# Joined column halves, a halved last tile and new order tables in a three-stage transformer block on one core

## The reference

```python
x = L0_attn_a_x                                   # (4, 512, 512) float32
# 1: sparse layer
attn = einsum('ds,td->st', w1, w2) * sparse_mask
x = x + gelu(einsum('bds,st->bdt', layernorm(x), attn) + b2)
# 2: clustered layer
n = layernorm(x)
dots = softmax(n @ centroids.T / 0.1);  hits = dots > 0.01
query_sel = any(hits, axis=1);  row_sel = any(hits, axis=0)[assignments]
x = x + where(query_sel[:, None] & row_sel[None, :], n @ weight.T + bias, 0)
# 3: attention with one head of 128
q, k, v = split(layernorm(x) @ Wqkv + bqkv)
x = x + softmax(q @ k.T / sqrt(128)) @ v @ Wo + bo
# 4: the clustered layer again, with the same weights
```

## Time and profile before

| | us |
|---|---|
| median of 3 runs | 284.21 |
| lowest, highest | 283.50, 284.87 |
| the profiled execution's own time | 283.48 |
| its span in the profile | 281.7 |
| TensorE busy | 271.4 (96%) |
| VectorE busy | 229.5 (81%) |
| ScalarE busy | 150.8 (54%) |
| GpSimd busy | 147.4 (52%) |

### The profile page before, as it was taken

One profiled execution on the slowest core, in us unless ns is written; L12 is line 12 of the kernel. 1 busy time (PEld: TensorE's weight loads), 2 busy tenths in 40 slices (PEclk: granted clock), 3 DMA queues, 4 the chain that ended last, 5 costly groups with the idle time before them and its releaser, 6 DMA issues.

```text
span 281.7 us, 4762 instructions
## 1 busy us (share of the span) xinstructions
PE 271.4 (96%) x1596; PEld 235.6 (84%) x1596; DVE 229.5 (81%) x458; ACT 150.8 (54%) x274; POOL 147.4 (52%) x186
## 2 busy tenths in 40 slices
PE   6999999999999999999799999999999999999893
PEld 5878888888888898789789999999889988898672
DVE  2889798968977958678799888889658796896996
ACT  5476747434757474264686665871653555356300
POOL 2233770485952554579999998671073005305820
PEclk9999999999999999999999999999999999999999
DMA  6985939000000000000000000000000000000087
GB/s 223 376 332 181 357 122 349 23 0 3 0 0 3 0 0 2 0 0 3 0 1 2 0 2 0 0 3 0 2 1 0 2 0 2 1 0 5 0 300 296
DMA packets 9976, 18.26 MB, mean 65 GB/s; under 512 B 1056, under 2 KB 1568, under 8 KB 9952
## 3 DMA queue, kind: packets, MB, share of 16 engines
q1 hardware_dynamic: 9952, 17.96, 18.0%
HBM read 13.76 MB, written 4.19 MB: 64 GB/s over the span
## 4 chain that ended last, share of the span: by engine, by line
PE 79%; POOL 8%; DVE 6%; issue 4%; ACT 1%; DVEq 1%; POOLq 0%; ACTq 0%
PE m_bank L864 60%; PE t_bank L955 11%; PE m_bank L1025 5%; POOL y_tok L480 3%; DVE x_tok L848 3%; POOL y_tok L493 2%; POOL rstd L431 1%; PE m_bank L856 1%; PE m_bank L915 1%; PE t_bank L961 1%; POOL ve L430 1%; DVE y_tok L841 1%; DVE odd_lo L707 1%; DVE st L700 1%; POOL nbias L434 1%
## 5 line engine op out<-in xcount | busy, mean ns | idle before, releaser
L700 DVE BATCH_NORM_STATS2 st<-x_tok 128x6 f32<-128x512 f32 x64 | 43.6, 681 | 0.5 <-DMA x_tok<-in_L_attn_a_x 0.4
L493 POOL TENSOR_TENSOR y_tok<-y_tok,x_tok 128x512 f32<-128x512 f32 x16 | 20.9, 1329 | 38.3 <-ACT y_tok L649 38.3
L864 PE MATMUL m_bank<-ffn_hi,even_hi 128*128 128x512 f32 x96 | 39.2, 408 | 0.0
L864 PE MATMUL m_bank<-ffn_lo,even_hi 128*128 128x512 f32 x96 | 37.6, 391 | 0.0
L864 PE MATMUL m_bank<-ffn_hi,even_lo 128*128 128x512 f32 x96 | 37.5, 391 | 0.0
L430 POOL TENSOR_SCALAR ve<-mv 128x1 f32<-128x1 f32 (+1 forms) x31 | 9.2, 297 | 39.3 <-DVE mv L701 37.7
L473 POOL TENSOR_TENSOR y_tok<-y_tok,bias_f 128x512 f32<-128x512 f32 x16 | 20.6, 1300 | 16.6 <-ACT y_tok L594 16.6
L864 PE MATMUL m_bank<-odd_hi,wqkv_hi 128*128 128x256 f32 x96 | 27.8, 290 | 1.1 <-ACT y_tok L594 1.1
L864 PE MATMUL m_bank<-odd_lo,wqkv_hi 128*128 128x256 f32 x96 | 27.1, 283 | 0.0
L864 PE MATMUL m_bank<-odd_hi,wqkv_lo 128*128 128x256 f32 x96 | 27.1, 282 | 0.0
L431 POOL TENSOR_TENSOR rstd<-ve,half 128x1 f32<-128x1 f32 (+1 forms) x31 | 23.6, 762 | 2.6
(11 more groups left out here) (163 smaller groups left out, 791.6 us busy)
## 6 DMA issues: line engine op xcount, KB each, us to landing
out<-x_tok SPq DMA_DIRECT2D x16, 256.0 KB, 2.3
x_tok<-in_L_attn_a_x SPq DMA_DIRECT2D x3, 1024.0 KB, 11.3
xn_odd<-in_L_attn_a_xt SPq DMA_DIRECT2D x2, 1024.0 KB, 6.1
w_raw<-in_L_attn_a_w SPq DMA_DIRECT2D x4, 256.0 KB, 4.2
y_tok<-in_L_attn_a_w SPq DMA_DIRECT2D x4, 256.0 KB, 4.4
x_tok<-in_L_attn_a_x SPq DMA_DIRECT2D x2, 512.0 KB, 6.6
y_tok<-in_L_attn_a_sparse_mask SPq DMA_DIRECT2D x1, 1024.0 KB, 9.2
xt_other<-in_L_ffn_weight SPq DMA_DIRECT2D x1, 1024.0 KB, 11.3
```

The source lines that it names most:

```text
L493: pool.tensor_tensor(y_tok[:, n, :], y_tok[:, n, :], x_tok[:, n, :], ALU.add).then_inc(done[kind], 1)
L700: link(dve.bn_stats(st[:, at % 2, :], x_tok[:, n, :]))
L864: ins = pe.matmul(bank, a, w, start=(first and n == 0), stop=(last and n == count - 1))
```

## The change

It does six things.

- For q, k and v of batches 1 to 3, pv of all batches, and the cluster products of batches 0 to 2 in both clustered stages, the two halves become one step `h01`: 12 (cluster: 8) products of 512 columns for 24 (16) of 256, waiting for all four tiles.
- The last dense tile, batch 3 tile 3 of stage 4, becomes two steps `dn4h` of 256 output columns, each with its own bank, `blend4h`, `outh` and store.
- All tables of TensorE, ScalarE, VectorE and GpSimd are new. SyncE's differs only in the last store.
- `WARM` is 4.
- `logit` waits for the count of `prob` that its own batch has in the table, since the two orders may differ.
- `rq` gets a leading dimension of 2, of which the second half is used; the `mT` names stand for no step.

```diff
-WARM = 6
+WARM = 4
...
 PE_ORDER = """
-T.v.0.0 k.1.h0 q.1.h0 q.1.h1 T.p.0.0 T.p.0.1 T.p.0.3 T.p.0.2 k.1.h1 v.1.h1 v.1.h0 sc.1.3 pv.0.h1 sc.1.1 T.x3.2.2
...
+k.1.h01 q.1.h01 T.p.0.3 T.p.0.1 T.p.0.2 v.1.h01 T.x3.2.0 T.x3.2.1 sc.1.0 sc.1.2 sc.1.1 T.x3.2.2 sc.1.3 T.x3.2.3
...
-store.2.2 store.2.3 store.3.0 store.3.1 store.3.2 store.3.3
+store.2.2 store.2.3 store.3.0 store.3.1 store.3.2 storeh.3.3.0 storeh.3.3.1
...
@@ -149,12 +149,12 @@
 PARTS = {"y1": KC, "dn2": KC, "dn4": KC, "cl2": 2, "cl4": 2, "q": 2, "k": 2, "v": 2, "pv": 2, "colmean": KC}
 T_KINDS = ("T", "tc", "bestT", "colmean")
-M_KINDS = ("last", "y1", "dn2", "dn4", "cl2", "cl4", "q", "k", "v", "sc", "pv", "wo", "mask")
+M_KINDS = ("last", "y1", "dn2", "dn4", "dn4h", "cl2", "cl4", "q", "k", "v", "sc", "pv", "wo", "mask")
 def tile_of(kind, key):
-    return () if kind == "colmean" else key[:-1] if kind in PARTS else key
+    return () if kind in ("colmean", "mT") else key[:-1] if kind in PARTS else key
 def products_order():
@@ -169,7 +169,7 @@
             first.add(at)
             rotating = [t for t in bank if (t[0] in T_KINDS) == (kind in T_KINDS)]
             bank[tile] = len(rotating)
-        taken[tile] += 1 if kind not in PARTS or kind == "colmean" else len(str(key[-1])) - 1
+        taken[tile] += 1 if kind not in PARTS or kind in ("colmean", "mT") else len(str(key[-1])) - 1
         if taken[tile] == PARTS.get(kind, 1):
             last.add(at)
     return first, last, bank
@@ -281,7 +281,7 @@
         csum = sb("csum", [P, TPB])
         crec = sb("crec", [P, TPB])
         qsel = sb("qsel", [P, 2, NT])
-        rq = sb("rq", [P, NT])
+        rq = sb("rq", [P, 2, NT])
         t_bank = [ctx.enter_context(nc.psum_tensor(f"t_bank{i}", [P, 512], F32)) for i in range(T_BANKS)]
         m_bank = [ctx.enter_context(nc.psum_tensor(f"m_bank{i}", [P, 512], F32)) for i in range(M_BANKS)]
@@ -354,6 +354,12 @@
                     b, t = key
                     sp.wait_ge(*done_at("out", (b, t)))
                     sp.dma_start(out_d[b, t * P:(t + 1) * P, :], x_tok[:, b * TPB + t, :]).then_inc(stored, 16)
+                    continue
+                if kind == "storeh":
+                    b, t, h = key
+                    cols = slice(h * D // 2, (h + 1) * D // 2)
+                    sp.wait_ge(*done_at("outh", key))
+                    sp.dma_start(out_d[b, t * P:(t + 1) * P, cols], x_tok[:, b * TPB + t, cols]).then_inc(stored, 16)
                     continue
                 what = key[0]
                 if what in ("w2", "w1"):
@@ -395,7 +401,7 @@
                     sp.wait_ge(*done_at("alo"))
                     sp.dma_start(wqkv_raw, rows_of(wqkv_d)).then_inc(ld[key], 16)
                     sp.dma_start(wo_raw, wo_d).then_inc(ld[key], 16)
-            sp.wait_ge(stored, 16 * NT)
+            sp.wait_ge(stored, 16 * sum(kind in ("store", "storeh") for kind, key in SP_STEPS))
         @block.gpsimd
         def _(pool):
@@ -791,8 +797,8 @@
                 elif kind == "logit":
                     stage, b = key
                     bank = bank_of("tc", stage, b)[:, :].rearrange("p (t h c) -> p t c h", t=TPB, h=2)
-                    if COUNT[kind][key] > 1:
-                        dve.wait_ge(done["prob"], COUNT[kind][key] - 1)
+                    if COUNT["prob"][key] > 1:
+                        dve.wait_ge(done["prob"], COUNT["prob"][key] - 1)
                     dve.wait_ge(*done_at("tc", key))
                     dve.tensor_reduce(out=cl[:, :, :], in_=bank, op=ALU.add, axis=AX.X).then_inc(done[kind], 1)
                 elif kind == "lmax":
@@ -815,7 +821,7 @@
                                            ALU.mult))
                     dve.wait_ge(chosen_done, COUNT[kind][key])
                     if stage == 4:
-                        dve.tensor_tensor(rq[:, b * TPB:(b + 1) * TPB], rstd[:, i:i + TPB], chosen, ALU.mult)
+                        dve.tensor_tensor(rq[:, 1, b * TPB:(b + 1) * TPB], rstd[:, i:i + TPB], chosen, ALU.mult)
                     if COUNT[kind][key] > 1:
                         dve.wait_ge(done[kind], COUNT[kind][key] - 1)
                     dve.tensor_tensor(best[stage][:, :, :], best[stage][:, :, :], cl[:, :, :],
@@ -838,8 +844,25 @@
                     dve.wait_ge(*done_at("dn4", key))
                     dve.wait_ge(*done_at("xb", key))
                     dve.wait_ge(*done_at("prob", (4, b)))
-                    dve.scalar_tensor_tensor(out=y_tok[:, n, :], in0=bank_of("dn4", *key)[:, :], scalar=rq[:, n:n + 1],
+                    dve.scalar_tensor_tensor(out=y_tok[:, n, :], in0=bank_of("dn4", *key)[:, :], scalar=rq[:, 1, n:n + 1],
                                              in1=y_tok[:, n, :], op0=ALU.mult, op1=ALU.add).then_inc(done[kind], 1)
+                elif kind in ("blend4h", "outh"):
+
+                    b, t, h = key
+                    n = b * TPB + t
+                    cols = slice(h * D // 2, (h + 1) * D // 2)
+                    if kind == "blend4h":
+                        dve.wait_ge(*done_at("dn4h", key))
+                        dve.wait_ge(*done_at("xb", (b, t)))
+                        dve.wait_ge(*done_at("prob", (4, b)))
+                        dve.scalar_tensor_tensor(out=y_tok[:, n, cols], in0=bank_of("dn4h", *key)[:, cols],
+                                                 scalar=rq[:, 1, n:n + 1], in1=y_tok[:, n, cols],
+                                                 op0=ALU.mult, op1=ALU.add).then_inc(done[kind], 1)
+                    else:
+                        dve.wait_ge(*done_at("mask", (4,)))
+                        dve.wait_ge(*done_at("blend4h", key))
+                        dve.copy_predicated(x_tok[:, n, cols], bank_of("mask", 4)[:, cols].bitcast(I32),
+                                            y_tok[:, n, cols]).then_inc(done[kind], 1)
                 elif kind == "out":
                     b, t = key
                     n = b * TPB + t
@@ -866,7 +889,7 @@
                 return ins
             freed_by = {"T": "lo", "tc": "logit", "bestT": "csel", "last": "mask_attn", "y1": "x1", "dn2": "ev2",
-                        "dn4": "blend4", "v": "vev", "sc": "exp", "pv": "olo", "wo": "x3"}
+                        "dn4": "blend4", "v": "vev", "sc": "exp", "pv": "olo", "wo": "x3", "dn4h": "blend4h"}
             def freed(kind, key):
@@ -921,8 +944,8 @@
                                              (w2t_hi[:, c, :], w2t_lo[:, c, :]))], first=False, last=False)
                 elif kind == "last":
                     i, = key
+                    rows_i = slice(i * P, (i + 1) * P)
                     c = KC - 1
-                    rows_i = slice(i * P, (i + 1) * P)
                     pe.wait_ge(*done_at("w2lo", (c,)))
                     pe.wait_ge(*done_at("w1lo", (c,)))
                     products(bank_of("last", i)[:, :], [((w1_hi[:, c, rows_i], w1_lo[:, c, rows_i]),
@@ -987,6 +1010,15 @@
                     if kind in ("y1", "dn2", "dn4", "sc", "wo"):
                         t = tile[1]
                         cols = slice(t * P, (t + 1) * P)
+                    if kind == "dn4h":
+                        t, h = key[1:]
+                        cols, outs = slice(t * P, (t + 1) * P), slice(h * D // 2, (h + 1) * D // 2)
+                        hi, lo = clustered_in(b)
+                        pe.wait_ge(*split("x4", b, [t]))
+                        ins = products(bank[:, outs], [((hi[:, c, cols], lo[:, c, cols]),
+                                                        (ffn_hi[:, c, outs], ffn_lo[:, c, outs])) for c in range(KC)])
+                        ins.then_inc(done[kind], 1)
+                        continue
                     if kind in ("y1", "dn2", "dn4"):
                         chunks = [int(c) for c in key[-1][1:]]
                     elif kind in PARTS:
```

168 lines of the change are left out of this document (84 added, 84 removed).

## The result

| | before | changed |
|---|---|---|
| median | 284.12 us (6 executions, the first three among them) | 286.87 us (285.69 to 288.18, 6 executions) |
| the profiled execution's own time | 283.48 | 285.69 |
| its span | 281.7 | 283.9 |
| TensorE busy | 271.4 | 269.5 |
| `mask.4` starts | 265.89 | 267.41 |

The account below looks back on a forecast made before the run. The end was taken as the time of `mask.4` (TensorE's work plus idle) plus 12.8 us of VectorE and 2.5 us of store. Six terms summed to -3.05 us: span 278.65, median 281.2 us, range 279.2 to 284.0.

Parts of the forecast that it names:

- term 4: Last cluster transpose to `mask.4`: VectorE's chain decides, stretch falls from 10.24 to 8.4 us, -0.5 us.
- term 3: Entry of the attention stage, 120 to 146 us: the 1.12 us wait on `ev2` goes, -1.0 us.
- Term 1: TensorE ahead of `mask.4`: 204 joined pairs save 0.0136 us each; with moved work, -2.15 us.
- term 2: Start: two warm-up calls fewer and the first dense stage reordered, -0.1 us, bounds -0.6 and +0.4.
- Term 5: Joined products wait for four transposed tiles instead of two: new waits, +0.4 us, bounds 0 and +1.5.
- Term 6: Tail behind `mask.4`: half `out` and blend steps on VectorE +0.2, extra store +0.1, together +0.3 us.
- The slower one: Rival, chance 0.07: joined products become serial points with 6.5 us of idle, giving 287.3 us.
- Waits eat the gain: Rival, chance 0.16: GpSimd sets the attention entry's pace, both collisions stay, new waits cost 1.2; 283.6 us.

Follow-up runs that it names:

- run 3: Changed kernel with every joined step written as its two halves side by side: 288.26 us, ratio 1.0144 against the kernel before.
- Run 2: Kernel before with four warm-up calls instead of six, nothing else: 283.95 us, ratio 0.9987.
- run 1: Changed kernel with six warm-up calls instead of four, nothing else: 286.66 us, ratio 1.010 against the kernel before.
- run 7: Changed kernel, attention entry: three GpSimd `rstd` steps moved ahead, waiting VectorE steps moved back, ScalarE's `norm.3.1.0` earlier: 285.81 us, ratio 1.0067 against the kernel before.
- run 9: Changed kernel, attention entry: three GpSimd `rstd` steps first, then `masked.2.0`; VectorE's `x2` steps moved, ScalarE's order kept: 286.29 us, ratio 1.0071 against the kernel before.
- run 6: Changed kernel with GpSimd's `xb.2.3` and `xb.2.2` held back and `blend4.2.2` behind two copies: 284.90 us, ratio 1.003 against the kernel before.
- run 12: Changed kernel with two product groups of `dn4.2.0` moved behind `tc.4.3` and `blend4.2.0` behind `lmax`: 284.39 us, ratio 1.0016 against the kernel before.
- run 8: Kernel before with the last dense tile in two halves, plus moves making room for them: 284.25 us, ratio 1.0003.
- run 5: Changed kernel timed again, no edit: 285.87 us, ratio 1.0076 against the kernel before.
- run 10: Changed kernel with `xb` additions held back, GpSimd's `rstd` steps first at the attention entry, and `dn4.3.0` groups ahead of `dn4.3.2`: 283.41 us, ratio 0.9974 against the kernel before.
- run 4: Kernel before with the same 19 tiles joined, each at its second half's place, order otherwise as before: 291.98 us, ratio 1.030.
- run 11: Kernel before with four warm-up calls, `xb.2.3` held until `csel`, `xb.2.0` moved ahead, and blends moved into gaps: 284.43 us, ratio 1.0006.

## Why the prediction was wrong, point by point

Two steps failed above all: term 4 had VectorE's chain ahead of `mask.4` too short, and term 3 took 1.0 us of idle time away at the entry of the attention stage, where 0.5 came. Between the forecast span (278.65) and the measured one (283.9) lie 5.25 us. By stretch, 1.7 of them lie in the chain, 1.65 from `mask.2` to `logit.4.3`, 1.4 ahead of the first `colmean` (scatter, and the wait for `rawlo`) and 0.4 behind `mask.4`. The median was missed by 0.4 more, by the clock.

**Term 1 (-2.15).** The price of a pair (0.0136 us) was right: run 3 measured 2.2 to 2.5 us where the count gives 2.45. So was the total of work: the table has -0.48, +0.27 and -1.36, and the tile that moved past the first `colmean` is -0.52; the rest is the 0.08 of one change from transposes to products (my parts add up to -2.17, not -2.15). Wrong was the step from "work ahead of `mask.4`" to time. The 0.52 became the wait of 0.64 to 0.70 us for `rawlo`. In term 2 I had weighed this lost filling against steps that run earlier, and put both together at 0.1. And 1.36 lay between `tc.4.3` and `mask.4`, where VectorE's chain decides; term 4 had reckoned with that, but with a chain short enough for the saving to pay. It was not, so all of it became idle time. Up to `mask.2` the work fell by 0.48 and the time by 0.42. Between `mask.2` and `tc.4.3` the joining saves 2.45, but the new order puts 2.72 us of other work there, for an end with less of it. The time there rose by 1.3: 0.27 is work, 0.56 idle (2.12 against 1.56, the two rows below, of before and of the changed kernel), and 0.46 I cannot place.

```profile
117.48:255.65 138.17, 136.61 (x923) 124.06 (x923) 115.08 (x231) 76.81 (x148) 79.06 (x98) 1.00 0.00 1
```

```profile
117.83:257.29 139.46, 137.34 (x755) 116.36 (x754) 115.64 (x232) 77.85 (x149) 82.12 (x101) 1.00 0.00 1
```

**Term 2 (-0.1).** Run 2 bounds the calls at 0 to -0.8, run 1 shows no difference. The start scatters by 1.5 us between traces, so neither bound is tested. With six calls, so with the same first product at 5.38, the first `colmean` comes at 18.24 in the new order (run 1) and 18.20 in before's: the reordered start gains nothing of its 0.52 us less work.

**Term 3 (-1.0; measured +0.5 of idle).** The wait on `ev2` went, but the term named the later `norm` of batch 1 as late next and then gave it 0.1 us (1.12 gone, 1.0 taken), as if GpSimd's inputs for it would keep their time while TensorE "arrives there 0.8 to 1.5 us earlier". The inputs of the last two tiles of the batch even came 0.2 and 0.75 us later, counted from `mask.2`: `bias2.2.2` (1.32) now stands among the `rstd` steps, and some of these steps stay long, `ve` with 0.78 instead of 0.22, as in the kernel before. My own rival had said that GpSimd sets the pace here; runs 7 and 9 agree, as each only moved the waits. That it is so stays the likely reading: no run here gives GpSimd less to do.

**Term 4 (-0.5).** This is the largest single piece. I put the stretch at 8.4 us, between 9.0 with both collisions and 6.9 without; it took 10.12. There are three collisions, not two, with 0.81, 1.13 and 1.06 us, 3.0 in all. The chain without them is 7.6 us from `tc.4.3` (run 6), and each costs what is left of the GpSimd addition that runs when the tiny step starts: nearly all of it here, less in run 12 (`ncmx` 0.39, `csel` 0.80). So it has to be read from the two orders, step by step, and not taken as a mean. The two orders show that GpSimd's `xb` have their inputs in this stretch, and nothing held them back.

The page "SBUF — State Buffer" of the Trainium skill (section "SBUF: two separate sides") has the rule: GpSimd and a VectorE operation in a two-port mode, or with two SBUF inputs, take the same port pair as an exclusive lock (the second case only against a GpSimd operation that reads SBUF, as these additions do), and the later one waits until the other's instruction is over. The rows agree: `ncmx` and `rq` have two SBUF inputs, `qsel` and `csel` read one and are held too (by the rule that would be the two-port mode, which no row shows), while the 128x512 blends, which read PSUM, keep their 0.75 beside the same additions.

**Term 5 (+0.4).** Nothing of it came: no joined product waits over 0.3 us, and TensorE shows no idle time from 150 to 255.

**Term 6 (+0.3; measured +0.68).** Half blends step by 0.38 and half copies too, as taken. VectorE waited 0.31 us for `dn4.3.0` at 272.70, and the last store took 0.21 longer in this trace (see the last point of this text). In the order before, the halves cost nothing measurable (run 8).

**Not in the forecast:** the clock. In the changed kernel and its variants with the same end (the first six executions and runs 1, 5, 7 and 9) 17 of 35 executions have a mean granted clock of 0.994 or less, in runs 6, 10 and 12 none of 36. (Run 3, with the same end and the halves not joined, has one of four, and it is no slower than the others.) It accounts for most of the spread, and in the first six, four of which have it, for about 1 us of the median. Without it the change is still slower, by about 1.5 us (285.65 in run 5 against 284.19).

**The rivals.** The slower one gave 287.3, close to 286.87, but by a mechanism that did not occur: joined products waited only in run 4, where the order was not made for them. "Waits eat the gain" named the right places and had 283.6, since it let the chain's stretch shrink to 9.0 us where 10.12 passed (it had two collisions, not three), and knew neither the wait at the start nor the clock.

## What to carry to other kernels

Price removed work by the stretch it leaves: where a chain on another engine is longer than the work beside it, less work is only more idle time. The fastest order here gives both the same length (run 10). A tiny VectorE step on the critical path wants GpSimd silent for its 0.2 us, and a wait on GpSimd gives it that when its result is not urgent. But the steps that move with it must still fit: in runs 6 and 11 the stretch behind grew by nearly as much as the chain had shrunk, or more, and only run 10 kept the gain. Ask of every pause on TensorE what clock comes behind it, and look at the clock of each execution before believing one profile.

## What the hardware did that I had not expected

- **The granted clock falls behind a stretch in which TensorE mostly waits, in some executions and not in others.** With 1.73 us of work in 265:269 (run 7) it was 0.50 from 269 on; with 1.25 in 148:151 (run 4), 0.57 for four microseconds. In run 5 TensorE worked 1.71 of 4 us in 264:268 and the clock stayed at 1.00. A fall costs TensorE about 1.5 us here, with products of 512 columns at 0.42 to 0.43 us instead of 0.227, and the end of the program 1.0 to 1.15 (runs 7 and 9). No single pause exceeded 2 us.
- **A GpSimd addition of 1.28 us holds a VectorE step of 0.16 us until its own end.** `qsel` started at 262.35 beside an addition from 262.34 to 263.62, and ended at 263.65. The delay is what is left of the addition: in run 12 `csel` started at 265.90 beside one from 265.33 to 266.62 and ended at 266.70.
- **The first products are spaced at 0.41 us or more instead of 0.23, for 1 to 10 spacings, with a granted clock shown as 1.00.** The number differs from trace to trace and was as high as 8 with six warm-up calls (run 8). The first `colmean` starts at 18.20 to 19.75 with it.
- **A smaller last store is not reliably a faster one:** from the last copy to the end pass 2.29 to 2.92 us in ten traces with a last store of 128 KB, 2.6 on the mean, and 2.51 to 2.52 in four with 256 KB.
